# Non-local block on one core: 512 moving columns per weight load in the query projection and in attention, and the split pieces of x on eight different 64-byte lines

## The reference, cut to what matters

```python
q = einsum('bchw,dc->bdhw', x, theta_w) + theta_b        # d = 256, n = 1024 positions
k = einsum('bchw,dc->bdhw', maxpool2(x), phi_w) + phi_b  # m = 256 positions
v = einsum('bchw,dc->bdhw', maxpool2(x), g_w) + g_b
p = softmax(einsum('bdn,bdm->bnm', q, k) * 256 ** -0.5, axis=-1)
vp = einsum('bdm,bnm->bdn', v, p)
out = einsum('bdhw,cd->bchw', vp, z_w) + z_b + x
```

## Time and profile before

| | |
|---|---|
| time, median of 3 | 2042.68 us (2042.04 to 2044.65) |
| span of the profiled execution | 2040.4 us |
| time beside the span: median less span | 2.3 us |
| matmuls | 17790 |
| granted TensorE clock | 1.000 of full |
| HBM traffic | 199 GB/s over the span |

### The profile page before, as it was taken

The page is one execution under the profiler, slowest core; times in us unless marked ns, Lnnn a source line. Parts: engine busy times, 40 slices in busy tenths (PEclk is TensorE's granted clock), DMA queues, the critical chain, the costliest instruction groups (busy, mean ns, idle before and its releaser), DMA issues.

```text
span 2040.4 us, 48999 instructions
## 1 busy us (share of the span) xinstructions
PE 2026.8 (99%) x17790; PEld 2024.5 (99%) x17790; DVE 1558.1 (76%) x2625; ACT 1300.0 (64%) x2228; POOL 1366.5 (67%) x828
## 2 busy tenths in 40 slices
PE   9999999999999999999999999999999999999998
PEld 9999999999999999999999999999999999999998
DVE  8878777787777877777877778777787777787777
ACT  6666666666566665666666666666666566666663
POOL 4577666776666766667766677666677666776663
PEclk9999999999999999999999999999999999999999
DMA  7565656746556565566565664656656556656554
GB/s 243 191 212 184 213 169 214 236 170 210 175 207 232 180 210 185 186 226 210 181 212 171 215 237 169 209 177 207 232 180 210 184 187 226 209 182 214 170 193 166
DMA packets 213963, 407.27 MB, mean 200 GB/s; under 512 B 12720, under 2 KB 17840, under 8 KB 213936
## 3 DMA queue, kind: packets, MB, share of 16 engines
q1 hardware_dynamic: 213792, 406.90, 59.0%
q10 hardware_dynamic: 144, 0.01, 0.0%
HBM read 272.64 MB, written 134.22 MB: 199 GB/s over the span
## 4 chain that ended last, share of the span: by engine, by line
PE 97%; DVE 2%; POOL 0%; DMA 0%; issue 0%; ACT 0%; SPq 0%; DVEq 0%; POOLq 0%
PE bank L967 97%; DVE x_top L755 0%; DVE pt_raw L736 0%; DMA x<-x 0%; DVE x_bot L755 0%; DVE pooled L708 0%; POOL att_lo L631 0%; POOL x_split_lo L613 0%; POOL att_f L626 0%; DVE x L755 0%; PE bank L974 0%; SPq L265 0%; DVE q_lo L714 0%; ACT att_hi L425 0%; DVE xp_lo L851 0%
## 5 line engine op out<-in xcount | busy, mean ns | idle before, releaser
L613 POOL TENSOR_TENSOR x_split_lo<-x,x_split_hi 128x1024 fp32r<-128x1024 f32 x255 | 614.6, 2417 | 248.4 <-ACT x_split_hi L386 226.7
L967 PE MATMUL bank<-x_split_hi,theta_hi 128*128 128x256 f32 x2048 | 565.8, 276 | 3.1 <-POOL x_split_lo L613 2.0
L967 PE MATMUL bank<-x_split_lo,theta_hi 128*128 128x256 f32 x2048 | 565.7, 276 | 0.0
L967 PE MATMUL bank<-x_split_hi,theta_lo 128*128 128x256 f32 x2048 | 565.7, 276 | 0.0
L967 PE MATMUL bank<-att_hi,z_hi 128*128 128x256 f32 x1792 | 495.4, 276 | 3.6 <-DVE x_bot L755 2.5
L967 PE MATMUL bank<-att_hi,z_lo 128*128 128x256 f32 x1792 | 494.9, 276 | 0.0
L967 PE MATMUL bank<-att_lo,z_hi 128*128 128x256 f32 x1792 | 494.9, 276 | 0.0
L736 DVE STREAM_TRANSPOSE pt_raw<-probs 32x256 f32<-32x256 f32 x1024 | 445.9, 435 | 18.4 <-ACT probs L489 1.8
L631 POOL TENSOR_TENSOR att_lo<-att_f,att_hi 128x768 fp32r<-128x768 f32 x191 | 282.6, 1487 | 159.4 <-ACT att_hi L425 159.4
L967 PEld LDWEIGHTS bank<-x_split_hi,theta_hi 128*128 128x128 f32 x2048 | 384.6, 188 | 3.5 <-issue 3.5
L967 PEld LDWEIGHTS bank<-x_split_hi,theta_lo 128*128 128x128 f32 x2048 | 384.6, 188 | 0.0
(11 more groups left out here) (76 smaller groups left out, 4390.0 us busy)
## 6 DMA issues: line engine op xcount, KB each, us to landing
x<-x SPq DMA_DIRECT2D x258, 512.0 KB, 3.9
x_top<-x SPq DMA_DIRECT2D x128, 512.0 KB, 7.0
out<-x_top SPq DMA_DIRECT2D x128, 512.0 KB, 3.3
x_bot<-x SPq DMA_DIRECT2D x126, 512.0 KB, 5.2
out<-x_bot SPq DMA_DIRECT2D x126, 512.0 KB, 6.6
x_top<-theta_wt SPq DMA_DIRECT2D x4, 256.0 KB, 5.4
x_top<-g_wt SPq DMA_DIRECT2D x4, 256.0 KB, 5.4
x_bot<-z_wt SPq DMA_DIRECT2D x4, 256.0 KB, 6.2
```

The costliest lines, as they stand in the source:

```text
L613: nc.gpsimd.tensor_tensor(flat(lo), flat(x_chunk(s, c)), raw(flat(hi)), ALU.subtract).then_inc(x_ready, 1)
L967: last = nc.tensor.matmul(dst, stationary(a), moving(b), start=start and n == 0, stop=stop and n == len(PRODUCTS) - 1, skip_group_check=re ...
```

## The change

Two things are edited. First, `project_q` and `attend` issue one matmul of 512 columns where two of 256 columns stood, with the same stationary tile; so a q chunk has 12 matmuls instead of 24, and attend 12 instead of 24. In `project_q` the start flag is now set for the whole bank at the first channel tile, and the stop flag at the last. Second, the tiles are allocated in another order. By the same reckoning as above the eight `xs` tiles begin at eight different places modulo 512 bytes: low 0 at 0, high 0 at 64, low 1 at 128, high 2 at 192, low 2 at 256, high 3 at 320, low 3 at 384, high 1 at 448. All other tiles that TensorE reads keep their place modulo 512, and the total size stays the same.

```diff
-        sb("pad_a", [P, 16], f32)
+        def piece_half(i, s):
+            return sb(f"x_split_{s}{i}", [P, KC, H], f32r)
+
+        xs = [[None, None] for _ in range(XS)]
+        xs[0][1] = piece_half(0, "lo")
+        bias = sb("bias", [P, NB], f32)
         att = [sb(f"att_{s}", [P, 7, HB], f32r) for s in ("hi", "lo")]
         k = [sb(f"k_{s}", [P, DT, M], f32r) for s in ("hi", "lo")]
         gw = [sb(f"g_{s}", [P, KT, D], f32r) for s in ("hi", "lo")]
-        xs = [[sb(f"x_split_{s}{i}", [P, KC, H], f32r) for s in ("hi", "lo")] for i in range(XS)]
         pt = [sb(f"pt_{s}", [P, MT, H], f32r) for s in ("hi", "lo")]
-        bias = sb("bias", [P, NB], f32)
+        xs[0][0] = piece_half(0, "hi")
         phi_bias = sb("phi_bias", [P, DT], f32)
         negmax = sb("negmax", [P, NT], f32)
+        xs[1][1] = piece_half(1, "lo")
         rowsum = sb("rowsum", [P, NT], f32)
         rowinv = sb("rowinv", [P, NT], f32)
-
-        sb("pad_b", [P, 32], f32)
+        xs[2][0] = piece_half(2, "hi")
+        sb("pad_b", [P, 16], f32)
+        xs[2][1] = piece_half(2, "lo")
+        sb("pad_c", [P, 16], f32)
+        xs[3][0] = piece_half(3, "hi")
+        sb("pad_d", [P, 16], f32)
         theta = [sb(f"theta_{s}", [P, KT, D], f32r) for s in ("hi", "lo")]
...
-        sb("pad_c", [P, 16], f32)
+        xs[3][1] = piece_half(3, "lo")
+        sb("pad_e", [P, 16], f32)
         phi = [sb(f"phi_{s}", [P, KT, D], f32r) for s in ("hi", "lo")]
+        xs[1][0] = piece_half(1, "hi")
...
-                        for h in range(2):
-                            last = product(q_banks(turn, s)[m][:, h * HB:(h + 1) * HB],
-                                           lambda a: theta[a][:, kt, m * P:(m + 1) * P],
-                                           lambda b: x_split(s, c)[b][:, i, h * HB:(h + 1) * HB], kt == 0 and h == 0, True, True)
+                        last = product(q_banks(turn, s)[m][:, :], lambda a: theta[a][:, kt, m * P:(m + 1) * P],
+                                       lambda b: x_split(s, c)[b][:, i, :], kt == 0, kt == KT - 1)
...
-                    for h in range(2):
-                        for mt in range(MT):
-                            last = product(att_banks(turn, s)[m][:, h * HB:(h + 1) * HB], lambda a: vt[a][:, mt, m * P:(m + 1) * P],
-                                           lambda b: pt[b][:, mt, h * HB:(h + 1) * HB], mt == 0, mt == MT - 1)
+                    for mt in range(MT):
+                        last = product(att_banks(turn, s)[m][:, :], lambda a: vt[a][:, mt, m * P:(m + 1) * P],
+                                       lambda b: pt[b][:, mt, :], mt == 0, mt == MT - 1)
```

## The result

The changed kernel takes 2070.34 us (median of 4, 2069.81 to 2070.64) against 2043.17 us for the kernel before in the same comparison: a ratio of 1.0132, 95% interval 1.0118 to 1.0146. I had forecast 2005 us, with a range up to 2034. The sign was wrong.

What follows compares the result with a forecast made beforehand. TensorE was taken as the bound, busy 99% in an almost unbroken chain. From a span of 2040.4 us, minus 42, plus 4, plus 0 gave 2002; with 2.3 us to the median, 2005 us, range 1995 to 2034 (8 in 10).

Steps and rivals of the forecast that it cites:

- the 6.7 ns: Loop, 256-column float32r matmul: time beside its columns, 113.3 less 106.7 ns, put down to a weight load not keeping up.
- X = 215.8: q projection and attention: forecast start-to-start time in ns of one 512-column matmul, replacing two starts of 226.7 ns in all.
- The two loads 110 ns apart: After a wait: first two weight loads start 110 ns apart, read as a load lasting about as long as 256 columns.
- The 2.4 ns of the zeros: Matmuls of zeros, 192 columns: 82.4 ns a step against 80 ns of columns, taken as the matmul's own cost.
- The 42 us of gain: q projection and attention: 3792 pairs on the chain gain 41.3 us, plus 1.0 us for slow prologue pairs.
- The entries: Narrow blocks following a 512-column one: 320 entries at 12 ns each, 4 us lost; bounds 0 and 35 us.
- The places of x: q matmuls with x tiles at eight distances from theta: cost taken as 0, upper bound 26 us.
- no gain: Rival, 7 in 100: float32 columns read no faster, 512 take twice 113.3 ns, time stays 2042 to 2045 us.
- 1157 GB/s: Moving-operand reading rate from 128 x 256 x 4 bytes in 113.3 ns, held to show the 614 GB/s limit doesn't apply.
- The slower rival: Rival, 8 in 100: loads beside the moving stream delay it at changed x places; 2062 to 2082 us, about 2070.
- The slow blocks: Rival, 15 in 100: 256-column blocks run half or all at the slow pace, costing 18 to 35 us; about 2025.
- the own price: Rival, 2 in 10: 6.7 ns belong to each matmul, 220.0 ns per wide one; gain 25 and 1.8 us, 2020 us.

Runs made afterwards that it cites:

- the wide-only kernel: 512-column matmuls in project_q and attend, all tiles at their old places, against the kernel before: 2069.06 us against 2042.58, ratio 1.0169.

## Why the prediction was wrong

The step that failed is "I take that as the reason for the 6.7 ns, and so take X = 215.8". The 6.7 ns beside 256 columns were not a load that couldn't keep up; they are what float32r columns cost in streaming, at least 13.3 ns for 512 of them: with 32 weight columns a wide matmul still took 231.1 ns, and no place got below 226.7. (Each of these still had a load before it; only its length is excluded as the cause.) The two loads 110 ns apart were a true reading that bears on 128-column matmuls only (111.8 ns). The 2.4 ns of the zeros were true too, for bf16; I carried a price over from one type to another because it fitted a model of the load, and gave the float32r row only 2 in 10.

Step by step: that TensorE bounds the kernel, that no seam tears and no engine becomes late, and the counts and the path (3840 pairs, 13950 matmuls) were right. The 42 us of gain were 0 at the best, and a loss of 20 us here, since X is 231.6 and 233.9 and not 215.8. The entries that I put at 4 us cost about 2 at the old places of x (0.2 ns on each of 5376 and 0.4 on each of 1536 matmuls in the wide-only kernel). The 7.5 us in the output projection are another thing, P3 and P4 in the slow pace throughout, and the new places of x bring them about. The places of x, which I put at 0 "since X is already near its columns", are worth 41 us with narrow matmuls; with wide ones they change X by 1.3 ns on the mean, and by chunk X is 228.9, 233.3, 232.2 and 232.0 ns, the difference between chunks that I had named as the sign that the place matters. That the place alone does not decide the pace of narrow matmuls, and the way of entry does too, was right.

Of the rivals, no gain had the right mechanism for the floor: 512 columns take twice what 256 take. Against it I had held 1157 GB/s. That excludes another limit and not this one, and the Trainium skill, in the section that I had cited for it ("SBUF — State Buffer", "A bandwidth-pool intuition that's wrong (but worth ruling out)"), gives the 614 GB/s for bf16, at 2 bytes an element. I should have kept the reading rate that the rows bounded as the likeliest. The slower rival had the right number, about 2070 us, and a moving stream delayed in steps at that, but from the wrong place: it blamed the new places of x and the loads beside the stream. The old places give 232.9 ns, more than the new ones, and narrow loads don't help. The slow blocks were in part there, one pair of output groups in three, though not with X = 215.8. In the own price the 1.8 us of prologue count 0.8 us of the 25 twice; its 2020 us stay.

What stays open is why the pace has two values. Shown is: both appear for the same tiles, at the same distance, with all else idle; what came before decides; with the places of the kernel before the loop came to its usual pattern from both paces of entry that occurred; and in three kernels the one product whose moving tile stands one line off the others modulo 256 bytes was the one whose pace differed, slow where the others were fast and fast where they were slow, and in the kernel with phi moved both of these one after the other. With x and pt moved two groups of moving tiles stand one line apart, and all narrow products are slow. That reads like a phase between the stream and something that turns with the address, but no run measured such a thing. No version faster than the kernel before was found. Width has nothing to give, since wide matmuls at their best equal two narrow ones at their fast pace; the 6.4 us of the key projection remain, and no run had all narrow products at the fast pace at once.

## What to carry to other kernels

Before merging matmuls to save a fixed cost, measure whether the cost is fixed: one block of the wide form, appended at the end of the kernel, would have told 227 to 233 ns from 216 for some 6 us of run time. Price a type by rows of that type, float32r not by bf16. And where TensorE is the bound in float32r, treat the order of tiles in SBUF as a parameter of its own that acts on the whole stream: moving the tiles of x slowed output groups that do not read x, and moving xp, phi and gw slowed nearly all products, so look at each product's distance between starts, not only at the one edited.

## What the runs showed of the hardware

A float32r matmul of 128 x 128 weights at full clock takes at best 113.3 ns for 256 columns, 226.7 for 512, and 176.7 for 384 at the one place tried; in bf16 512 columns take 215.7. Above this stand surpluses of up to 8 ns. They depend on the place of the moving tile relative to the weights, with a period of 256 bytes, and for 256 columns also on what came before. Between the best and the worst order of tiles tried with the same 17790 matmuls lie 2043 and 2104 us, 3%.
